# RWKV-style mixing with a product-key expert layer: eight gathers ahead in two tiles, an earlier last projection, and a finish in halves

## The reference

```
xn  = layernorm(x)
# recurrent part
k, v, r = (mix of xn and xn shifted by one token) @ Wk.T, Wv.T, Wr.T
s   = (sigmoid(r) * wkv(-exp(time_decay), time_first, k, v)) @ Wo.T
# feed-forward part
q   = xn @ Wq.T                       # 2 halves x 4 heads x 64
top 8 of 128 keys for each half, top 8 of the 64 pairs  -> 32 expert indices per token
down, up = down_embed[idx], up_embed[idx]          # tables of 16384 x 1024
w   = silu(<xn, down>) * softmax(scores)           # 32 numbers per token
g   = silu( silu(xn @ Wg.T) * (xn @ Wu.T) @ Wd.T  +  sum_j w_j * up_j )
out = x + s * g
```

## Time and profile before

| what | us |
|---|---|
| median of 3 runs | 1945.49 (1944.62 to 1960.31) |
| the profiled execution, its time | 1954.08 |
| its span on the slowest core (core 1) | 1952.5 |
| spans of the eight cores | 1929.4 to 1952.5 |
| PE / DVE / ACT / POOL busy on core 1 | 1310.2 / 1247.2 / 935.2 / 842.0 |
| bytes moved by core 1's DMA | 607.94 MB, mean 311 GB/s |

### The profile page before, as it was taken

One profiled execution on the slowest core, in us unless ns is written; L12 is line 12 of the kernel. 1 busy time (PEld: TensorE's weight loads), 2 busy tenths in 40 slices (PEclk: granted clock), 3 DMA queues, 4 the chain that ended last, 5 costly groups with the idle time before them and its releaser, 6 DMA issues.

```text
span 1952.5 us, 23343 instructions; the slowest of 8 cores (1929.4 to 1952.5 us)
## 1 busy us (share of the span) xinstructions
PE 1310.2 (67%) x5504; PEld 546.3 (28%) x5504; DVE 1247.2 (64%) x2531; ACT 935.2 (48%) x1509; POOL 842.0 (43%) x776
## 2 busy tenths in 40 slices
PE   1179968996899689970762376568665777766665
PEld 1134323332333233330320122223222332222222
DVE  3758888878887888761442366555555656556665
ACT  3545433543354345431554555444454544545554
POOL 0033334334332433334332366555555655555563
PEclk9999989997899899995895588889888998888899
DMA  9899999999999999999999989999999999999996
GB/s 274 253 318 312 317 306 316 312 324 306 313 310 316 304 316 315 323 315 306 312 300 327 305 288 327 326 314 313 324 326 324 319 322 325 333 323 328 330 304 228
DMA packets 229111, 607.94 MB, mean 311 GB/s; under 512 B 37872, under 2 KB 70640, under 8 KB 226928
## 3 DMA queue, kind: packets, MB, share of 16 engines
q0 software_dynamic: 73888, 268.73, 42.9%
q1 hardware_dynamic: 91008, 268.48, 42.2%
q10 hardware_dynamic: 64080, 69.24, 12.4%
HBM read 510.15 MB, written 96.47 MB: 311 GB/s over the span
## 4 chain that ended last, share of the span: by engine, by line
DMA 68%; PE 10%; POOL 8%; issue 8%; DVE 4%; ACT 2%; SPq 1%; DVEq 0%; POOLq 0%; ACTq 0%
DMA arena<-upE 35%; DMA arena<-tabb,expi 25%; POOL arena L419 4%; POOL arena L405 4%; DMA arena<-x_nat 3%; DMA arena<-wdT 2%; PE ps_a L576 2%; PE ps_b L576 2%; DVE arena L865 1%; PE ps_b L436 1%; DMA arena<-woT 1%; PE ps_c L436 1%; PE ps_a L552 1%; SPq L324 1%; ACT arena L1092 1%
## 5 line engine op out<-in xcount | busy, mean ns | idle before, releaser
L419 POOL DMA_INDIRECT arena<-tabb,expi x512 | 541.5, 1058 | 491.0 <-PE ps_d L576 149.8
L1092 ACT ACTIVATE arena<-arena 128x1024 bf16<-128x1024 bf16 x384 | 404.1, 1053 | 442.6 <-DVE arena L904 438.1
L405 POOL CAST arena<-arena 128x1024 bf16<-128x1024 f32 x256 | 298.7, 1167 | 593.8 <-DMA arena<-downE 356.9
L904 DVE TENSOR_TENSOR arena<-arena 128x1024 bf16<-128x1024 bf16 x384 | 264.4, 695 | 365.6 <-DMA arena<-tabb,expi 280.4
L436 PE MATMUL ps_b<-arena 128*128 128x512 bf16 x1024 | 253.1, 391 | 34.1 <-ACT arena L1011 34.1
L436 PE MATMUL ps_c<-arena 128*128 128x512 bf16 x1024 | 249.4, 387 | 17.7 <-DVE arena L812 17.7
L576 PE MATMUL ps_a<-arena 128*128 128x512 bf16 x384 | 110.2, 439 | 162.7 <-DVE arena L865 162.7
L576 PE MATMUL ps_d<-arena 128*128 128x512 bf16 x320 | 105.4, 489 | 163.6 <-DVE arena L865 163.6
L897 DVE SCALAR_TENSOR_TENSOR arena<-arena 128x1024 bf16<-128x1024 bf16 x128 | 156.3, 1221 | 38.4 <-DMA arena<-tabb,expi 37.7
L1011 ACT ACTIVATE arena<-ps_b 128x512 bf16<-128x512 f32 x128 | 73.8, 596 | 216.5 <-PE ps_b L436 174.9
L436 PE MATMUL ps_a<-arena 128*128 128x512 bf16 x512 | 132.7, 408 | 57.1 <-ACT efac L994 36.0
(11 more groups left out here) (99 smaller groups left out, 1671.0 us busy)
## 6 DMA issues: line engine op xcount, KB each, us to landing
arena<-downE SPq DMA_DIRECT2D x128, 512.0 KB, 10.8
arena<-upE SPq DMA_DIRECT2D x128, 512.0 KB, 10.9
tabb<-arena SPq DMA_DIRECT2D x256, 256.0 KB, 9.3
arena<-x_nat SPq DMA_DIRECT2D x32, 512.0 KB, 9.8
arena<-wgS ACTq DMA_DIRECT2D x32, 512.0 KB, 10.3
arena<-wuS ACTq DMA_DIRECT2D x32, 512.0 KB, 11.4
h_scr<-arena ACTq DMA_DIRECT2D x64, 256.0 KB, 14.4
arena<-wdT SPq DMA_DIRECT2D x32, 512.0 KB, 11.8
```

What stands on the lines that cost most here:

```text
L405: e.tensor_copy(out=tout[s], in_=ring[s]).then_inc(pool_cast, 1)
L419: e.indirect_dma_start(out=gslot[n % NSLOT], out_offset=None, in_=d_tabb, in_offset=IndirectOffsetOnAxis(ap=expi[:, n:n + 1], axis=0)).the ...
L904: e.tensor_tensor(out=pdot[q % 3], in0=gslot[slot][:, 0:1024], in1=xnl[w % 2], op=ALU.mult).then_inc(dv_prod, 1)
L1092: e.activation(out=pdot[q % 3], in_=pdot[q % 3], func=AF.Copy, accum_out=dots[:, g * GS + x:g * GS + x + 1]).then_inc(ac_dots, 1)
```

## The change

Three edits. (1) In tiles 0 and 1 a gather waits for `pe_up` >= n - 7 (`NAHEAD` = 8); from tile 2 on for n - 15 as before. (2) In the last tile `go` is 5: the eight chunks of the output projection stand in groups 5 and 6 (they stood in 6 and 7). (3) The end of the last tile is split into two halves of 512 columns: the up matmuls of its last group run all four picks of the first half, then all four of the second; ACT's silu, DVE's multiply and add, and SP's store are two instructions each, the first set released by the first half.

```diff
+NAHEAD = 8
...
-            go = 6 - max(0, 2 * (w - t - 1))
+            go = 6 - max(0, 2 * (w - t - 1)) if w < NT - 1 else 5
...
         def store_out(t):
             e.wait_ge(dv_out, t + 1)
-            e.dma_start(out=d_out[ts(t), :], in_=ot[t % 2]).then_inc(st_out[t % 2], 16)
+            if t < NT - 1:
+                e.dma_start(out=d_out[ts(t), :], in_=ot[t % 2]).then_inc(st_out[t % 2], 16)
+                return
+            for i in range(2):
+                e.wait_ge(dv_out, t + 1 + i)
+                e.dma_start(out=d_out[ts(t), ts(i, 512)], in_=ot[t % 2][:, ts(i, 512)]).then_inc(st_out[t % 2], 16)
...
-                if n >= NSLOT:
-                    e.wait_ge(pe_up, n - NSLOT + 1)
+                ahead = NAHEAD if t < 2 else NSLOT
+                if n >= ahead:
+                    e.wait_ge(pe_up, n - ahead + 1)
...
                 e.wait_ge(dv_diag, NG * w + g + 1)
+                if w == NT - 1 and g == NG - 1:
+                    for n in range(2):
+                        for i in range(GS):
+                            j = g * GS + i
+                            slot = (w * 32 + j) % NSLOT
+                            mm = e.matmul(ps_e[w % 3][:, ts(n, 512)], diag[g % 2][:, ts(i)],
+                                          gslot[slot][:, 1024 + n * 512:1536 + n * 512], start=False,
+                                          stop=(i == GS - 1))
+                            if n == 0 and i == GS - 1:
+                                mm.then_inc(pe_up, GS)
+                        if n:
+                            mm.then_inc(pe_up, 1)
+                    break
...
+        def finish_last():
+            t = NT - 1
+            e.wait_ge(pe_wo, t + 1)
+            for i in range(2):
+                sl = ts(i, 512)
+                e.wait_ge(ac_fin, t + 1 + i)
+                e.tensor_tensor(out=ot[t % 2][:, sl], in0=ot[t % 2][:, sl], in1=ps_o[:, sl], op=ALU.mult).then_inc(dv_fm, 1)
+                e.wait_ge(dv_fm, t + 1 + i)
+                e.tensor_tensor(out=ot[t % 2][:, sl], in0=ot[t % 2][:, sl], in1=xt[t % 4][:, sl],
+                                op=ALU.add).then_inc(dv_out, 1)
...
-        finish(NT - 1)
+        finish_last()
...
-        final(NT - 1)
+        e.wait_ge(pe_wd, NT)
+        e.wait_ge(st_out[(NT - 1) % 2], 16 * ((NT - 1) // 2))
+        for i in range(2):
+            e.wait_ge(pe_up, 32 * NT + i)
+            e.activation(out=ot[(NT - 1) % 2][:, ts(i, 512)], in_=ps_e[(NT - 1) % 3][:, ts(i, 512)],
+                         func=AF.Silu).then_inc(ac_fin, 1)
```

More of the change, by code:

```diff
@@ L389, in sync_prog @@
         for i in range(2):
-            e.wait_ge(st_out[i], 16 * 8)
+            e.wait_ge(st_out[i], 16 * (8 + i))
     def gpsimd_prog(e):
```

## The result

| | us |
|---|---|
| before, median of 6 runs | 1946.7 (1944.62 to 1960.31) |
| changed, median of 6 runs | 1994.12 (1986.34 to 2006.32) |
| ratio changed / before | 1.0233, 95% interval 1.0202 to 1.0264 |
| profiled execution of the changed kernel, its time | 2006.32 |
| its span on the slowest core (core 3) | 2004.8 |

The kernel became slower by 2.3%: about 47 us and not the 21 forecast, and the time lies outside the range. The direction held, the size did not.

A forecast was written before the change was run, and what follows sets the result against it. The kernel was taken as bound by DMA bytes, so idle DMA counts. Gather loop +24 us and tail -3 gave +21 on the 1945.49 median: 1967 us, own range 1954 to 1983 (0.62), wider range 1943 to 1983.

The forecast's parts named there:

- The turn, 6.7 us + L = 13.5: Gather loop of tiles 0 and 1, one group's products to the next's: fixed terms 6.7 us plus L of 6.8.
- L: Landing time of a group's last gather: bounds 5.8 and 11.6 us, taken as 6.8, near the light end.
- Six turns, one step kept, one turn of 16.7, three of 13.5: Tiles 0 and 1, group by group: +9.1 us, step kept at 10.7, then +6.1 and +11.5.
- U(1,2): POOL's pace mark for tile 1, group 2; the step to it was forecast as 16.7 us, with L = 10: +6.1.
- The second sum, 36 us of idle DMA: Idle DMA at the start, tile 0, boundary and tile 1: 36 us less the 12 of before, +24, the value taken.
- the first sum: Steps of tiles 0 and 1 added, 9.1 - 1 + 6.1 + 11.5: +25.7 us at the start of the steady part.
- The third rival, a loaded loop: Gather loop: L = 9 in nine turns adds 2.2 us each, +20 on the forecast, 1980 to 1990; chance 0.08.
- The boundary, -1: Tile 0 to tile 1: fewer gathers queued shorten ACT's 22.9 us wait for SP's loads, by 0 to 6.5 us; -1 taken.
- the second rival: Weight loads at ACT's wait and later come 13 us sooner, no longer behind gathers: 1930 us; chance 0.10.
- Repayment: Part of a rival (-3 to +8 us, chance 0.20): pausing cores leave bandwidth to others; doubted, as all would pause together.
- From U(1,5) on, 0: From tile 1, group 5, POOL meets tile 2's picks with the old wait: 0 us, bounds -9.6 and +3.4.
- The tail, -3: End of the last tile: earlier projection -2.0 us, halves -1.1; -3 us taken, from -1 to -4.

## Why the prediction was right in direction and wrong in size

- *That the kernel is bound by bytes, so that idle DMA is the measure.* Held. The steady part did not change, and the loss is where the DMA share fell.
- *That the limit of eight closes a loop with four gathers in flight, because of DVE's order.* Held, and shown: the order alone takes the loss away at the same limit, and with 12 there is no loss to be told either.
- *The turn, 6.7 us + L = 13.5.* **This is the step that failed.** In tile 0 it was 16.0 us on core 3. The lines of one turn on DVE and POOL of core 3:

```profile
946.38 0.69 DVE L936 TENSOR_TENSOR arena<-arena 128x1024 bf16<-128x1024 bf16 x1 [0.93 <-DMA arena<-tabb,expi]
946.99 1.28 DVE L832 TENSOR_TENSOR arena<-arena,ps_c 128x512 bf16<-128x512 bf16 x2
...
948.45 0.69 DVE L885 TENSOR_TENSOR arena<-c_identb,wfin 128x512 bf16<-128x512 bf16 x1
...
962.16 0.69 DVE L936 TENSOR_TENSOR arena<-arena 128x1024 bf16<-128x1024 bf16 x1 [1.15 <-DMA arena<-tabb,expi]
...
954.66 0.94 POOL L426 DMA_INDIRECT arena<-tabb,expi  x1 [0.27 <-issue]
```

| term | forecast | tile 0 | alone (all eight, tile 2 on) |
|---|---|---|---|
| last product to the end of the diagonals | 0.9 | 2.1 | 0.9 |
| to the first gather | 1.5 | 1.9 | 1.9 |
| three more issues | 3.6 | 3.6 | 3.6 |
| landing L | 6.8 | 7.5 | 6.1 |
| the product | 0.7 | 0.7 | 0.7 |
| turn | 13.5 | 15.8 | 13.2 |

  The columns are one turn each: 947.07 to 962.85 here, 1417.06 to 1430.22 in the run with eight everywhere. Half of the 2.3 us that this turn missed by is work that the sum left out. The two hidden products stand in DVE's list ahead of the diagonals; the prediction described `hidden` as PE's pace of the loop before, but did not put its 1.3 us into the new loop. The run with `hidden` behind the diagonals gives roughly that back. 0.4 us is read as the PE clock. PE on core 3, and the windows of 949 to 953 and 953 to 960 us:

```profile
949.28 3.56 PE L596 MATMUL ps_a<-arena 128*128 128x512 bf16 x8 [6.95 <-DVE arena L885]
...
949.00:953.00 4.00, 3.71 (x10) 1.39 (x11) 0.14 (x1) 0.60 (x1) 1.68 (x2) 0.54 0.12 13
953.00:960.00 7.00, 6.78 (x32) 2.83 (x30) 1.93 (x3) 2.40 (x4) 2.06 (x3) 1.00 0.84 266
```

  After 6.95 us of idle PE starts at its lower level (0.54, 1.2 GHz): the eight up matmuls take 3.56 us, and the first two of them release the first gather. The 1.5 us of before was read at a group that took 1.89 us, at full clock. The first group of the kernel before is the other case: there too the matmuls took 3.57 us, and from the end of the diagonals to the gather at 930.05 were 1.9 us.

```profile
927.45 0.69 DVE L865 TENSOR_TENSOR arena<-c_identb,wfin 128x512 bf16<-128x512 bf16 x1
...
928.29 3.57 PE L576 MATMUL ps_a<-arena 128*128 128x512 bf16 x8 [55.82 <-DVE arena L865]
```

  The windows of core 3 show the hole: while PE works the DMA engines have nothing to do (share 0.12, 13 GB/s). L was 0.7 too low: the light end was chosen for a place where weight loads and hidden stores still run beside the gathers.
- *Six turns, one step kept, one turn of 16.7, three of 13.5.* The sum of the steps was 29.1 us too low, and the turn is behind most of it: 15.2 us in the six turns of tile 0, 4.6 at U(1,2) and 5.2 in the three turns after it, beside 1.3 at U(0,7) and 2.9 at the boundary. The three turns of tile 1 took 15.2 us each, with an L of 6.2 to 9.6 us beside the weight loads. At U(1,2), 21.3 us for 16.7, L was 14.2 (from the last issue at 1085.17 to its product at 1099.32) and not 10. An upper row stood in the prediction (L = 11.6), and only this one turn was given a value near it.
- *The second sum, 36 us of idle DMA.* It was 65.8 us on the mean of the cores. That it came to the size of the first sum was no confirmation, since its 17 us for tile 0 were worked out from the same turn of 13.5. Its 8 us ahead of U(0,0) did not come as such: on core 3 the DMA share over 920 to 934 was 0.81, 2.7 us of idle.
- *The third rival, a loaded loop, came nearest.* It was given 0.08. Its time, 1980 to 1990, is closest to the 1994 measured, but only in part for its reason: L was 7.5 in the turn of tile 0 above and not 9, and in tile 1 it lay on both sides of 9; the hidden products and the PE clock are in none of the rivals. The value near the lightest row was taken because there would be less in flight, though the closed loop takes away only gathers and leaves every weight load where it was.
- *The boundary, -1.* ACT's wait behind the last hidden store went from 22.9 us to this, on core 3:

```profile
1065.61 1.06 ACT L1109 ACTIVATE arena<-arena 128x1024 bf16<-128x1024 f32 x1 [20.31 <-DMA arena<-wdT]
```

  It gave 2.6 us of it. The step as a whole grew by 1.9 us instead of shrinking by 1. U(1,0), which lies within it, came 14.6 us behind U(0,7) (1041.43 to 1055.99) and had come 7.2 behind it before (1012.66 to 1019.89): with the limit of eight it stands behind the products of the gathers that U(0,7) released. The Wd loads of tile 1 did land sooner, before and then after:

```profile
L348 SPq DMA_DIRECT2D arena<-wdT x12: 327/328/333, 1040.6 to 1074.2; - x12
...
DMA to landing us min/median/max: 8.8/11.3/12.8
```

```profile
L349 SPq DMA_DIRECT2D arena<-wdT x12: 327/328/333, 1066.7 to 1104.5; - x12
...
DMA to landing us min/median/max: 7.5/8.5/14.5
```

  So the mechanism of the second rival exists: the median load landed in 8.5 us and not 11.3. It paid back little beyond the 2.6 us above, since behind the boundary the groups wait for their gathers. DVE's longest waits on core 3 between 1080 and 1115 are 10.91 and 9.85 us, both for the first gather of a group.
- *Repayment.* By idle share the loss would be 54.4 us on the mean of the cores; the mean span grew by 43.0 (1943.2 to 1986.2), and by 46.4 with the tail's 3.4 us taken out. Some 8 us were paid back, 3.6 of them behind U(1,5). Part of it shows as a higher rate while the engines are busy: over tile 1's second half the share is 0.59 at 204 GB/s, which is 346 GB/s at a full share, against 322 / 0.99 = 325 in the steady part of before; but over tile 0 it is only 240 / 0.75 = 320 beside 310 / 0.98 = 316. The prediction's reason against repayment was that all cores would pause together. That is not borne out: U(0,0) lies between 914.0 and 933.6 us, each counted from its own core's start, a spread of more than one turn. The cores' clocks are not tied to each other in the traces, so the overlap of their pauses can't be read directly. The Trainium skill ("HBM Reference", the text on the two cores of a domain) says that a core streaming alone gets more than its share of a pair. That fits what little shows in the rates, but no run here switched a neighbour off, so this cause is argued and not shown.
- *From U(1,5) on, 0.* Held within a few us: 846.4 us against 848.6 on the cores shown, 841.6 against 845.2 on the mean of all.
- *The tail, -3.* Held: -3.4, of it 1.7 from each edit; it had been forecast as 2.0 and 1.1. Edit 3 gives more because of the store, whose gain the forecast had left at nothing: the last one, of 256 KB, was issued at 2002.4, 2.4 us before the end of the span, where the 512 KB of before took 2.9 (1949.60 to 1952.5). Up to that issue edit 3 gave about the 1.1 us forecast.

## What to carry to other kernels

A limit on how far ahead a load may run is not a number of buffers: follow the wait through the program order of every engine in between, and count how many groups are in flight between two of its releases. If that is only one, the loop's period is the sum of everything in it, so list each instruction that stands in it on each engine, at the clock which the engine will then have, and with the landing time of the traffic that stays. And in a kernel bound by bytes, relieving the queue for other loads was worth little by itself here; look for the place where the DMA engines stand idle, and free the engine that holds up the issue there.

## What the runs showed of the hardware that was not expected

With all eight cores running and little else queued, four overlapping gathers of 0.525 MB (128 rows of 4 KB) landed 5.7 to 6.3 us after their issue (the run with eight everywhere, 1400 to 1440), and groups of four gathers, issued 1.2 us apart, kept the DMA engines at a share of 0.54 only, the tiles' own loads and stores included (1200 to 2500). The granted PE clock stood near its lower level where PE ran one group of up matmuls in each turn of 13 to 17 us and little else (0.53 at 1110 to 1160 in the changed kernel). By the rows above this lengthened the very loop that had made PE idle, by some 0.4 us a turn.
